# Four transformer-like layers on one core: minus the row maximum enters through a spare row of q's low half, and the residual moves ahead of two low halves on VectorE

## The reference, cut to what matters

```
xn  = ln(x) * (1 + scale1) + shift1
q, k, v = split(xn @ w_qkv + b_qkv)          # 16 heads of 18 columns; q and k are normalised per head in blocks 0 and 2
attn = softmax(q @ k.T / sqrt(18)) ; o = attn @ v
x   = x + gate1 * (o @ w_proj + b_proj)
xn2 = ln(x) * (1 + scale2) + shift2
x   = x + gate2 * (gelu(xn2 @ w1 + b1) @ w2 + b2)
```

## Time and profile before

| | |
|---|---|
| median of 3 runs | 4510.08 us (4502.52 to 4513.27) |
| the profiled execution | 4508.88 us, of which 4507.2 us are the span of the instructions |
| mean granted clock of PE | 0.965 |
| a steady slot of layers 0 and 1 | 40.3 us (scoresT(0) of one to scoresT(0) of the next: 1006.40 to 1046.69) |
| a steady slot of layer 2 | 44.7 us (qkv(0) at 3611.61 to qkv(0) at 3656.30) |

### The profile page before, as it was taken

One profiled execution on the slowest core, in us unless ns is written; L12 is line 12 of the kernel. 1 busy time (PEld: TensorE's weight loads), 2 busy tenths in 40 slices (PEclk: granted clock), 3 DMA queues, 4 the chain that ended last, 5 costly groups with the idle time before them and its releaser, 6 DMA issues. The chain is left out here.

```text
span 4507.2 us, 124159 instructions
## 1 busy us (share of the span) xinstructions
PE 4177.3 (93%) x46073; PEld 3554.6 (79%) x46073; DVE 3633.4 (81%) x7651; ACT 2300.9 (51%) x3892; POOL 1113.7 (25%) x2051
## 2 busy tenths in 40 slices
PE   6764899999999999999999999999999999999998
PEld 4653788888888888888888888887888888888886
DVE  5775888898888997777777777789888888888885
ACT  1212555555555555555555555555555555555553
POOL 1102222222222233222222222233222222222212
PEclk8576999999999999999999999999999999999999
DMA  3101111101111111111110111111010111101010
GB/s 80 23 1 55 30 28 31 31 25 31 27 31 29 27 46 54 30 31 29 30 31 25 31 28 31 32 46 49 23 31 24 29 28 25 28 25 28 25 26 20
DMA packets 122213, 141.80 MB, mean 31 GB/s; under 512 B 14414, under 2 KB 117748, under 8 KB 122080
## 3 DMA queue, kind: packets, MB, share of 16 engines
q1 hardware_dynamic: 121936, 139.75, 11.8%
q10 hardware_dynamic: 144, 0.22, 0.0%
HBM read 110.87 MB, written 29.06 MB: 31 GB/s over the span
## 5 line engine op out<-in xcount | busy, mean ns | idle before, releaser
L1023 DVE TENSOR_REDUCE mx<-S 128x4 f32<-128x1024 f32 x768 | 903.0, 1217 | 174.3 <-PE S L1265 166.8
L758 ACT ACTIVATE pT<-S 128x1024 f32<-128x1024 f32 x768 | 745.5, 1023 | 369.1 <-PE S L1293 369.0
L706 ACT ACTIVATE hf<-M 128x512 f32<-128x512 f32 (+1 forms) x480 | 267.0, 556 | 736.9 <-DVE hl L1014 389.0
L620 POOL TENSOR_SCALAR hh<-hf 128x512 fp32r<-128x512 f32 (+1 forms) x480 | 282.0, 588 | 830.8 <-ACT hf L706 781.8
L1293 PE MATMUL S<-qT,kT 32*128 32x256 f32 x9216 | 425.1, 295 | 17.0 <-ACT pT L758 13.9
L1306 PE MATMUL A<-pT,V 128*32 128x256 f32 x6144 | 412.8, 386 | 25.1 <-ACT pT L758 25.1
L1293 PEld LDWEIGHTS S<-qT,kT 32*128 32x128 f32 x9216 | 328.6, 184 | 87.9 <-issue 46.9
L1200 PE MATMUL A<-wqkv_hi,xh 128*128 128x288 f32 x1152 | 283.6, 328 | 92.8 <-DVE x L1070 90.1
L1345 PE MATMUL M<-xh,w_hi 128*128 128x256 f32 x1728 | 364.2, 292 | 1.2 <-POOL xh L594 1.2
L1384 PE MATMUL M<-w_lo,hh 128*128 128x288 f32 x1728 | 353.0, 304 | 0.0
L1345 PE MATMUL M<-xh,w_lo 128*128 128x256 f32 x1728 | 344.4, 280 | 0.0
(11 more groups left out here) (245 smaller groups left out, 9862.0 us busy)
## 6 DMA issues: line engine op xcount, KB each, us to landing
mid<-xbo SPq DMA_DIRECT2D x64, 288.0 KB, 4.0
xld<-mid SPq DMA_DIRECT2D x64, 288.0 KB, 3.7
xa<-mid SPq DMA_DIRECT2D x64, 288.0 KB, 3.6
gA<-gates SPq DMA_DIRECT2D x96, 144.0 KB, 3.3
gM<-gates SPq DMA_DIRECT2D x96, 144.0 KB, 3.6
xld<-in_x_dram SPq DMA_DIRECT2D x32, 288.0 KB, 3.8
xa<-in_x_dram SPq DMA_DIRECT2D x32, 288.0 KB, 3.5
out_dram<-xbo SPq DMA_DIRECT2D x32, 288.0 KB, 2.2
```

Source lines behind the costliest of these rows:

```text
L620: pool.tensor_scalar(hh[:, 2 * f:2 * f + m, :].rearrange("p m c -> p (m c)"), hf[:, f % 3, 0:m * T], 1.0, 0.0, ALU.mult, ALU.add).then_inc ...
L706: act.activation(hf[:, f % 3, 0:c], MBANK[f % 2][:, 0:c], gelu(n)).then_inc(s["m_hf"], 1)
L758: act.activation(pT[:, g % 2, 2 * h:2 * h + 2, :], S[:, 2 * h:2 * h + 2, :], ACT.Exp, scale=float(HD) ** -0.5).then_inc(s["a_ex"], 1)
L1023: dve.tensor_reduce(mx[:, p, :, :], S[:, r:r + 2, :].rearrange("p a (t k) -> p a t k", t=NT), AX.X, ALU.max).then_inc(s["a_mx"], 1)
```

## The change

The fourth term of `A_scoresT` goes, and with it `pick`, `pickf` and the four affine selects that made them. Instead, column 18 of each head's 32-column slot of k is set to one, once, so that row 18 of each slot of transposed k (high half) is one; row 18 of q's low half, which was zero, receives minus the maximum, so that the second term (k high x q low) adds it. `A_negmax` writes one copy instead of four, in two instructions, its columns ordered so that each row tile's four heads are neighbours; `A_turn_max` transposes 16 columns; `A_shift` copies 16 rows and then issues four DMAs from ACT's queue, each of 4 KB from four partitions to one row of `qT`. `A_scoresT` waits for the four DMAs (`a_nmd`, 64) instead of for the copy. On PE `A_turn_max` moves ahead of the last eight matmuls of down0. On DVE `A_x1` and `A_max` 4 and 5 move ahead of `M_hl` 1 and 2, and `A_x1` runs as three loops over the two halves (multiplies, adds, statistics) in place of one.

```diff
 def A_shift(n):
     wait(act, "a_nmT", n, 1)
-    act.activation(nmT[:, :], S[:, 3, 0:T], ACT.Identity).then_inc(s["a_nmc"], 1)
+    act.activation(nmT[:, :], S[0:H, 3, 0:T], ACT.Identity).then_inc(s["a_nmc"], 1)
+    wait(act, "a_nmc", n, 1)
+    constant_wait(act)
+    for a in range(4):
+        row = SLOT * a + HD
+        act.dma_start(qT[row:row + 1, 1, :, :].bitcast(F32), nmT[QUADS * a:QUADS * (a + 1), :].bitcast(F32)).then_inc(s["a_nmd"], 16)
...
 def A_negmax(n):
-    dve.tensor_scalar(nm4[:, :, :, 0:H], mx[...].unsqueeze(2).broadcast_to([P, NT, 4, H]), -1.0, None, ALU.mult).then_inc(s["a_nm"], 1)
+    for b in range(2):
+        op = dve.tensor_scalar(nm[:, :, 2 * QUADS * b:2 * QUADS * (b + 1)]..., mx[...][:, b, :, :, :], -1.0, None, ALU.mult)
+    op.then_inc(s["a_nm"], 1)
...
 def A_x1(n):
     for i in range(NT):
         wait(dve, "a_pr", n, i + 1)
         dve.tensor_tensor(x1[:, i, :], ABANK[i][:, 0:D], gA[:, :], ALU.mult).then_inc(s["a_prd"], 1)
+    for i in range(NT):
         wait(dve, "a_prd", n, i + 1)
         dve.tensor_tensor(x1[:, i, :], x1[:, i, :], xa[:, i, :], ALU.add).then_inc(s["a_x1"], 1)
+    for i in range(NT):
         wait(dve, "a_x1", n, i + 1)
         constant_wait(dve)
         dve.bn_stats(stM[:, i, :], x1[:, i, :]).then_inc(s["m_bn"], 1)
...
 # DVE's slot
     A_max(p, 2); A_max(p, 3)
-    M_hl(m, 1); M_hl(m, 2)
     A_x1(a)
     A_max(p, 4); A_max(p, 5)
+    M_hl(m, 1); M_hl(m, 2)
     M_hl(m, 3); M_hl(m, 4)
...
 def A_scoresT(n, g):
     if g == 0:
-        wait(pe, "a_nmc", n, 1)
+        wait(pe, "a_nmd", n, 64)
...
-            for j in range(4):
+            for j in range(3):
                 for a in range(4):
-                    keys = (kT[rows, 0, g, at], kT[rows, 0, g, at], kT[rows, 1, g, at], pick[rows, g, :])[j]
-                    queries = (qT[rows, 0, g, :], qT[rows, 1, g, :], qT[rows, 0, g, :], nmT[rows, :])[j]
+                    keys = (kT[rows, 0, g, at], kT[rows, 0, g, at], kT[rows, 1, g, at])[j]
+                    queries = (qT[rows, 0, g, :], qT[rows, 1, g, :], qT[rows, 0, g, :])[j]
...
 # PE's slot
-    down0(16, 27)
+    down0(16, 19)
     A_turn_max(p)
+    down0(19, 27)
     qkv(5)
```

More of the change, by code:

```diff
@@ L48 @@
     a_sq=1, a_hs=1, a_nrm=1, a_v=2, a_T=4, a_qhi=2, a_khi=2, a_qlo=2, a_klo=2, a_S=8, a_mx=8,
-    a_nm=1, a_nmT=1, a_nmc=1, a_ex=8, a_pv=4, a_o=2, a_oT=2, a_on=4, a_nT=2, a_oh=2, a_ol=2,
+    a_nm=1, a_nmT=1, a_nmc=1, a_nmd=64, a_ex=8, a_pv=4, a_o=2, a_oT=2, a_on=4, a_nT=2, a_oh=2, a_ol=2,
     a_pr=2, a_prd=2, a_xa=16, a_x1=2, a_warm=2,
@@ L126, in build @@
         oh, ol = (sb(f"o_{h}", [P, FULL, T], F32R) for h in ("hi", "lo"))
-        nm4 = sb("nm4", [P, NT, 4, SLOT])
-        nmT = sb("nmT", [P, T], F32R)
+        nm = sb("nm", [P, NT, H])
+        nmT = sb("nmT", [H, T], F32R)
         wst = [sb(f"wst{i}", [P, F]) for i in range(2)]
-        pickf = wst[0][:, 0:QUADS * P].rearrange("p (q c) -> p q c", q=QUADS)
-        pick = sb("pick", [P, QUADS, P], F32R)
         pT = sb("pT", [P, 2, 4, 512])
@@ L391, in swap_load @@
             else:
-                sp.wait_ge(set_done, 14)
+                sp.wait_ge(set_done, 8)
             if len(ap.shape) == 3:
@@ L533, in constants @@
                 pool.memset(V[:, :, :, :], 0.0).then_inc(set_done, 1)
-                pool.memset(nm4[:, :, :, :], 0.0).then_inc(set_done, 1)
-                pool.memset(pickf[:, :, :], 0.0).then_inc(set_done, 1)
+                pool.wait_ge(set_done, 6)
+                pool.memset(V[:, :, :, 0:1], 1.0).then_inc(set_done, 1)
+                pool.memset(ks[:, :, :, HD:HD + 1], 1.0).then_inc(set_done, 1)
                 pool.wait_ge(set_done, 8)
[L537 to L544, removed]
             def A_mod(n):
@@ L1029, in A_negmax @@
                 wait(dve, "a_mx", n, PAIRS)
-                dve.tensor_scalar(nm4[:, :, :, 0:H], mx[:, :, :, :].rearrange("p q a t -> p t (q a)").unsqueeze(2).broadcast_to([P, NT, 4, H]),
-                                  -1.0, None, ALU.mult).then_inc(s["a_nm"], 1)
+                for b in range(2):
+                    op = dve.tensor_scalar(nm[:, :, 2 * QUADS * b:2 * QUADS * (b + 1)].rearrange("p t (x q) -> p q x t", x=2),
+                                           mx[:, :, :, :].rearrange("p (q b) x t -> p b q x t", b=2)[:, b, :, :, :], -1.0, None, ALU.mult)
+                op.then_inc(s["a_nm"], 1)
             def A_oraw(n, i):
@@ L1095, in slot @@
                 if p is not None and a is None:
-                    dve.wait_ge(set_done, 14)
+                    dve.wait_ge(set_done, 8)
                 if a is not None and m is None:
@@ L1148, in slot @@
                     A_max(p, 3)
-                if m is not None:
-                    M_hl(m, 1)
-                    M_hl(m, 2)
                 if a is not None:
@@ L1156, in slot @@
                     A_max(p, 5)
+                if m is not None:
+                    M_hl(m, 1)
+                    M_hl(m, 2)
                 if m is not None:
@@ L1272, in A_turn_max @@
                 for t in range(NT):
-                    op = pe.transpose(S[:, 3, t * P:(t + 1) * P], nm4[:, t, :, :].rearrange("p r h -> p (r h)"), ident[:, :])
+                    op = pe.transpose(S[0:H, 3, t * P:(t + 1) * P], nm[:, t, :], ident[:, :])
                 op.then_inc(s["a_nmT"], 1)
@@ L1287, in A_scoresT @@
                     at = slice(i * P, (i + 1) * P)
-                    for j in range(4):
+                    for j in range(3):
                         for a in range(4):
                             rows = slice(SLOT * a, SLOT * (a + 1))
-                            keys = (kT[rows, 0, g, at], kT[rows, 0, g, at], kT[rows, 1, g, at], pick[rows, g, :])[j]
-                            queries = (qT[rows, 0, g, :], qT[rows, 1, g, :], qT[rows, 0, g, :], nmT[rows, :])[j]
-                            op = pe.matmul(S[:, a, i * T:(i + 1) * T], keys, queries, start=(j == 0), stop=(j == 3))
+                            keys = (kT[rows, 0, g, at], kT[rows, 0, g, at], kT[rows, 1, g, at])[j]
+                            queries = (qT[rows, 0, g, :], qT[rows, 1, g, :], qT[rows, 0, g, :])[j]
+                            op = pe.matmul(S[:, a, i * T:(i + 1) * T], keys, queries, start=(j == 0), stop=(j == 2))
                 op.then_inc(s["a_S"], 1)
@@ L1484, in slot @@
                     if a is None:
-                        pe.wait_ge(set_done, 14)
+                        pe.wait_ge(set_done, 8)
                     A_turn_qk(p)
```

## The result

The median is 5263.89 us (4 runs, 5255.08 to 5269.45) beside 4508.49 us for the kernel before in the same rounds (4502.52 to 4513.27): a ratio of 1.1672 with a 95% interval of 1.1651 to 1.1692, slower by 755 us. The forecast was 4989, with a range up to 5120: the direction holds, the size doesn't. The profiled execution took 5255.08 us, 5253.4 of them span, at a mean granted clock of 0.899 (0.965 before).

A forecast was written before the change was run, and what follows sets the result against it. PE, busy 93%, was taken as the bound. To 4508.9 us came 358 us of slots (64 x 3.9 + 30 x 3.6) and 122 us of clock (94 x 1.3): 4989 us, range 4830 to 5120.

The forecast's parts named there:

- M_hl 1 and gelu 4: DVE's new order starts gelu 4 4.60 us late, so PE idles 3.8 us ahead of qkv(2), about 4 in layer 2.
- The old 0.91 us: PE's wait ahead of qkv(0) for the residual's multiply, 0.91 us a slot, goes because the multiply moves earlier.
- First fall of the clock: PE's clock falls behind the idle stretches of 3.8 and 4 us in nearly every slot, costing 1.3 us each.
- 0.5 us of waiting for the negation: PE reaches the earlier transposes at 2026.61 and waits to 2027.1 for DVE's negation, 0.5 us.
- The transfers: Four ACT issues 0.37 us apart and 1.7 us landing leave PE idle 1.5 us ahead of scoresT(0).
- The second fall of the clock: Clock falling again behind the gap ahead of scoresT(0); not in the forecast, kept as a rival at 0.11.
- 1.5 us is under the 2.19 that did nothing: Argument against a second fall: the 1.5 us transfer gap is shorter than a 2.19 us gap that didn't lower the clock.
- the rival: Clock falls behind the second gap as well, 1.4 us in each of 94 slots: 5120 us, chance 0.11.
- Fourth term: Dropping scoresT's fourth term takes eight groups of 0.12 us off PE, 0.96 us a slot, 92 us over 96 slots.

The follow-up runs named there:

- order_alone: Kernel before with only the new DVE order (residual as three loops, A_max 4 and 5 ahead of M_hl 1 and 2): 4931.6 us, ratio 1.0943.
- one_back: Kernel after with M_hl 1 alone put back ahead of the residual, M_hl 2 staying behind A_max 5: 4789.2 us, without an interval.
- order_back: Kernel after with M_hl 1 and 2 put back ahead of the residual on DVE: 4826.5 us, ratio to before 1.0709.
- neither: Kernel after with the old order of M_hl and residual and no transfers, three terms left: 4456.5 us, ratio to before 0.9888.
- late_store: Kernel after with SP's store and loads in layer 2 held back until the four transfers have landed: 5174.8 us, ratio 1.147.
- two_queues: Kernel after with two of the four transfers issued from SP's queue and two from ACT's: 5173.4 us, ratio 1.1478.
- multiply_first_row: Kernel after with only the residual's two multiplies ahead of M_hl 1 and 2, and transfers on two queues: 4656.8 us, ratio 1.0334.
- one_transfer: Kernel after with one of the four transfers and a wait for it alone: 4922.5 us, ratio 1.0916.

## Why the prediction was wrong

Its steps, by the profiled execution: 5255.1 measured, 4989 forecast, 266 us missing.

- *M_hl 1 and gelu 4: right to a few hundredths.* From qkv(0) the prediction put M_hl 1 at 3.80, gelu 4 at 4.58 and qkv(2) at 6.84; the trace has 3.79, 4.57 and 6.82. The idle time ahead of qkv(2) is 3.61 (forecast 3.8), ahead of `R_turn` 3.81 ("about 4"). order_alone and one_back show the cause. The old 0.91 us did go.
- *First fall of the clock: right, a little small.* From qkv(0) to the transposes the forecast has 11.75 without clock and without the 0.5 us of DVE; the trace has 13.28, so 1.53 in layer 1, against 1.3. In layer 2, from `R_turn` on, 12.88 against 11.30, 1.58.
- *0.5 us of waiting for the negation: didn't come.* PE lost more time at the low clock than DVE was late; PE's wait there is under 4 us in the whole run. It is there wherever the order is undone (22.7 us in order_back and in neither).
- *The transfers: mis-sized.* The copy is where it was put, and ends as forecast. But the issues start 0.6 apart and not 0.37, so the last one starts 0.74 later; from there to PE it is 1.92 instead of 1.8. That this half came so close is partly luck: the row it rests on, 1.7 us over three transfers, reads 3.3 in the kernel after. Transposes to scoresT(0): 4.64 against 3.8 in layer 1, +0.84. In layer 2 it is 6.05, +2.25, of which late_store and the rows of SP show the store and the loads as the cause of more than half. I took the issue of the nearest row on ACT's queue, 128 partitions wide, and no row shows a transfer from four partitions to one.
- *The second fall of the clock: the step that failed.* The prediction set it aside with "1.5 us is under the 2.19 that did nothing" and gave the rival 0.11. The gap wasn't 1.5 but 2.25, and behind 2.25 and 2.28 us the clock of the next 3 us was 0.57 and 0.50. As a rule the argument doesn't hold either: order_back's and late_store's gaps of one length fell in some slots and not in others. From scoresT(0) to qkv(0) a slot took 29.57; 40.3 less the 10.24 of the earlier trace rows, the 0.91 and the 0.96 would make 28.19, so the fall cost 1.38 us in layers 0 and 1, just the rival's price. (two_queues, which mostly holds its clock there, takes 28.08 for the same stretch as a median of layer 1: 1.49.) In layer 2 the same sum gives 2.35: from scoresT at 4248.25 to the next `R_turn` at 4283.83 are 35.58, against 44.7 - 13.61 (its `R_turn` to scoresT) - 0.96 + 3.1 = 33.23.
- *Fourth term: right.* scoresT is 0.95 us shorter in the run with neither part, against 0.96.

The differences, in the 64 slots of layers 0 and 1: 0.23 + 0.84 + 1.38 - 0.5 = 1.95 us, 125 us; in the 30 of layer 2: 0.28 + 2.25 + 2.35 = 4.88 us, 146 us. Together 271, for the 266 that are missing. About 159 of them are the second fall, 121 the transfers. The longer transfers brought the second fall: with issues at the price of the row I used, the gap would have stayed at 1.5 us, and two_queues, whose gap is 1.47 in the slot shown, fell in 6 of the 64 of layers 0 and 1 where the kernel after fell in 60. multiply_first_row, with the same gap and none for gelu 4, holds a granted clock of 1.00 (windows 1000 to 1500 and 2100 to 2900).

What stays open: what besides a gap's length decides whether the clock falls behind it, why the low stretches of two_queues last longer than those of one_transfer, and what the 1.4 us of a fall would be in a slot where PE isn't full. The transposes ahead of down0's last eight matmuls and the residual's three loops were not run by themselves; with three terms, the two are part of the 50 us of neither.

## What to carry to other kernels

An instruction that only feeds an engine with slack can still be the one that sets the pace, if an in-order list behind that engine ends at the bottleneck: follow the consumer's list (gelu, table, copy, bank) to the end before anything is put ahead of the producer. Move only the part that releases the wait (two multiplies, 0.73 us) and leave the rest where it is. On a core whose PE is nearly full, count a new idle gap twice, once as waiting and once as the low clock behind it, and when the forecast hangs on a gap's length being under one that was seen to be harmless, give the fall more than a small chance: one harmless gap is no limit.

## What the runs showed of the hardware

- A DMA of 4 KB from four partitions of SBUF to one row of another SBUF tensor held ACT's queue for 580 ns at least, and as median over 384 of them, where the loads and stores on SP's queue shown above took 0.34 to 0.40 us:

```profile
L741 ACTq DMA_DIRECT2D qT<-nmT x384: 580/580/1198, 430.1 to 5172.3; - x192
```

- Such a small transfer suffers from large ones under way: with a store and two loads of 144 to 288 KB at the same time, PE got its data 1.2 us later (3.5 to 2.4 us of wait when they were held back).
- How long PE idled didn't by itself tell whether its clock fell. It fell behind gaps of 2.07 us and up in 92 of 96 slots here, and behind 2.29 us (median) in 62 of 64 slots of late_store, but behind 2.36 us in only 5 of 32 of its layer 2; 2.19 us in the kernel before left it at full speed. Behind some 1.5 us it fell in 6 of 64 slots each of two_queues and multiply_first_row (layers 0 and 1). The time lost by a fall was 1.4 to 1.6 us in layers 0 and 1 and about 2.4 behind the second gap of layer 2.
- Doing useless matmuls in the idle time gave back 270 us of 755: PE ran them where it had idled, and its clock stayed up.
